# A graph layer's second and third matrix in parts of the TensorE array, by sets of four node tiles

## What is computed

```python
def gnn(x, edge_src, edge_dst, w, W1, W2, W3):      # W1 64x256, W2 32x64, W3 256x32
    agg = segment_sum(x[edge_dst], edge_src)
    y = agg + w * x
    h = relu(y @ W1.T)
    h = relu(h @ W2.T)
    h = relu(h @ W3.T)
    return h + x

x = x + gnn(layernorm(x), ...)
xn = layernorm(layernorm(x)) * gamma + beta
logits = xn @ Wr + br ; top 2 of 8, softmax of the two
for e in range(8): y += (gelu(xn @ W1[e] + b1[e]) @ W2[e] + b2[e]) * w_full[e]
out = x + y
```

## Time and profile before

| | us |
|---|---|
| median of 3 runs | 478.48 |
| lowest and highest | 477.6, 479.87 |
| span of the profiled execution, first to last instruction | 472.4 |
| third stage, first L1141 to L1224 | 157.13 to 216.15 |
| TensorE busy over the span | 380.4 (81%) |
| VectorE, ScalarE, GpSimd busy | 294.7, 222.6, 135.4 |

### The profile page before, as it was taken

The page is one execution under the profiler, slowest core; times in us unless marked ns, Lnnn a source line. Parts: engine busy times, 40 slices in busy tenths (PEclk is TensorE's granted clock), DMA queues, the critical chain, the costliest instruction groups (busy, mean ns, idle before and its releaser), DMA issues.

```text
span 472.4 us, 12881 instructions
## 1 busy us (share of the span) xinstructions
PE 380.4 (81%) x4344; PEld 346.1 (73%) x4345; DVE 294.7 (62%) x704; ACT 222.6 (47%) x351; POOL 135.4 (29%) x241
## 2 busy tenths in 40 slices
PE   0895598999998889980449999999999999999200
PEld 0684498999998667770349999999999999999100
DVE  2886998999994753568945444445444444444853
ACT  2475576888885274560025444444444444443000
POOL 3050000000000500000054665665666665653200
PEclk9987589999999977875559999999999999999755
DMA  9620299999999269930011222212222222215899
GB/s 202 154 54 3 40 183 199 214 220 222 216 222 200 63 241 362 375 116 0 0 58 58 77 70 72 72 67 67 75 69 73 72 67 67 75 60 135 207 228 310
DMA packets 112696, 62.15 MB, mean 132 GB/s; under 512 B 86625, under 2 KB 106743, under 8 KB 112544
## 3 DMA queue, kind: packets, MB, share of 16 engines
q1 hardware_dynamic: 101168, 41.80, 36.6%
q0 software_dynamic: 6272, 14.93, 10.2%
q10 hardware_dynamic: 5232, 5.12, 3.7%
HBM read 27.70 MB, written 13.64 MB: 88 GB/s over the span
## 4 chain that ended last, share of the span: by engine, by line
PE 70%; DMA 9%; DVE 8%; ACT 5%; issue 4%; SPq 3%; POOL 0%; ACTq 0%; DVEq 0%; POOLq 0%
PE psum L918 20%; PE psum L929 19%; PE psum L790 9%; PE psum L781 7%; DMA w_sb<-pair_rows 3%; PE psum L837 3%; PE psum L859 3%; PE psum L907 2%; DMA at<-cts 2%; DMA b_rows<-in_L_ffn_b_dram 2%; PE psum L721 1%; DMA pair_rows<-yb,scol 1%; SPq L288 1%; PE psum L712 1%; ACT cts L591 1%
## 5 line engine op out<-in xcount | busy, mean ns | idle before, releaser
L918 PE MATMUL psum<-xgT,w_now 128*128 128x128 f32 x832 | 103.2, 278 | 0.0
L918 PEld LDWEIGHTS psum<-xgT,w_now 128*128 128x128 f32 x832 | 98.8, 195 | 0.2 <-issue 0.2
L929 PE MATMUL psum<-w_sb,hT 128*128 x416 | 98.4, 380 | 0.0
L591 ACT CAST cts<-psum 128x1000 bf16<-128x1000 f32 x100 | 78.4, 815 | 23.7 <-PE psum L781 23.3
L929 PEld LDWEIGHTS psum<-w_sb,hT 128*128 128x128 f32 x416 | 75.1, 190 | 8.3 <-issue 0.3
L679 ACT ACTIVATE hT<-up 128x512 f32<-128x512 f32 x52 | 32.8, 630 | 97.7 <-DVE up L1347 97.7
L790 PE MATMUL psum<-z,at 125*128 (+1 forms) x1875 | 71.0, 195 | 3.2 <-DMA at<-cts 3.2
L668 ACT COPY w_now<-w_sb 128x1024 f32 x52 | 54.4, 1046 | 34.5 <-DVEq L1312 21.9
L790 PEld LDWEIGHTS psum<-z,at 125*128 125x128 bf16 x1875 | 65.9, 100 | 3.8 <-DMA at<-cts 2.1
L1347 DVE TENSOR_TENSOR up<-psum,b1T 128x512 f32<-128x512 f32 x52 | 36.0, 692 | 47.8 <-PE psum L918 47.8
L492 POOL DMA_INDIRECT pair_rows<-yb,scol x52 | 52.0, 999 | 46.9 <-issue 33.6
(11 more groups left out here) (228 smaller groups left out, 347.8 us busy)
## 6 DMA issues: line engine op xcount, KB each, us to landing
w_sb<-in_L_ffn_W_dram SPq DMA_DIRECT2D x2, 4096.0 KB, 20.4
token_rows<-tok SPq DMA_DIRECT2D x5, 560.0 KB
tok<-pair_rows SPq DMA_DIRECT2D x5, 560.0 KB
w_sb<-pair_rows SPq DMA_DIRECT2D x5, 560.0 KB
out_dram<-res ACTq DMA_DIRECT2D x5, 560.0 KB
res<-in_x_dram ACTq DMA_DIRECT2D x3, 560.0 KB
res<-in_x_dram SPq DMA_DIRECT2D x2, 560.0 KB
b_sb<-in_L_ffn_b_dram SPq DMA_DIRECT2D x1, 1024.0 KB, 23.8
```

What stands on the lines that cost most here:

```text
L591: act.copy(cts[:, par, :, d0:d0 + nw * WD].rearrange("p h (b d) -> p b h d", b=nb), psum[:, bank:bank + nb, 0:wb * WC].rearrange("p b (d h ...
L918: last = pe.matmul(psum[:, j % 2, c * P:(c + 1) * P], w1_now[:, j % 2, k, c * P:(c + 1) * P], xgT[:, j % 2, k, :], start=(k == 0), stop=(k ...
L929: last = pe.matmul(psum[:, 4 + j % 2, 0:D], hT[:, j % 2, k, :], w2_sb[:, ds(e, 1), k, :].rearrange("p a h -> p (a h)"), start=(k == 0), st ...
```

## The change

The 25 tiles go in seven sets, six of four tiles and one of one, in place of five groups of five. In a set:

- the second layer is four matmuls of 125 columns, one for each tile; each has the 64x32 weights and writes its own 32 rows of PSUM bank 4 (rows 0 to 31, 32 to 63, ...), so each uses its own 32 columns of the array;
- one ReLU reads these 128 rows x 125 columns (before: 32 rows x 375 and x 250);
- the third layer is four matmuls of 256 columns, each with 32 rows of `h2T` and the same 32 rows of `gW3T`, each into its own bank (6, 7, 0, 1); `gW3T` now holds the matrix four times, one below the other; VectorE waits for the last of the four;
- the residual takes two tiles in an instruction (125x512), from two banks;
- tokens go two tiles to a bank, through the banks 2 and 5, and are copied two at a time (128x500);
- `deviation2` of set k-1 stands ahead of `relu_y` of set k+1 on ScalarE.

`top_two` takes 24 tiles and then one. At the start POOL copies `gW3` four times side by side (a new instruction that waits for the loads and stands ahead of the constants that follow on POOL), in place of two memsets; TensorE waits for it before its first transpose, and turns 128 columns of it in place of 32.

```diff
+SL = P // F2
+SETS = -(-NT // SL)
...
-        H3 = (6, 7, 0)
-        TURN = (1, 2)
-        ALL_BUT_LAST = NT - G
+        H3 = (6, 7, 0, 1)
+        TURN = (2, 5)
+        MLP = 4
+        ALL_BUT_LAST = (SETS - 1) * SL
...
-            pool.memset(gW3T[:], 0.0).then_inc(c_more, 1)
-            pool.memset(h2T[:].rearrange("p t n -> p (t n)"), 0.0).then_inc(c_more, 1)
+            pool.wait_ge(L["small"], 64)
+            pool.tensor_copy(gW3_sb[:], gW3_in[:].unsqueeze(2).broadcast_to([P, KD, SL, F2])).then_inc(gW3_spread, 1)
...
+            def relu_h2(k):
+                n = len(sets[k]) * F2
+                act.wait_ge(h2_psum, k + 1)
+                act.activation(h2T[0:n, :], psum[0:n, MLP, 0:T], ACT.Relu).then_inc(h2_sb, 1)
...
+            def copy_tokT(k):
+                for i, ts in enumerate(pairs_of(k)):
+                    n, t0 = len(ts), 2 * i
+                    act.wait_ge(tokT_psum, 2 * k + i + 1)
+                    act.copy(tokT[:, :, t0:t0 + n, :], psum[:, TURN[i], 0:n * KD * T].rearrange(
+                        "p (t k n) -> p k t n", t=n, k=KD)).then_inc(tokT_sb, 1)
...
+            pe.wait_ge(gW3_spread, 1)
...
+            def second_layer(k):
+                pe.wait_ge(yT_sb, k + 1)
+                for i in range(len(sets[k])):
+                    last = pe.matmul(psum[i * F2:(i + 1) * F2, MLP, 0:T], gW2T[:], y1T[:, i, :], start=True, stop=True)
+                last.then_inc(h2_psum, 1)
+
+            def third_layer(k):
+                pe.wait_ge(h2_sb, k + 1)
+                if k >= 1:
+                    pe.wait_ge(h3_used, 2 * k)
+                for i in range(len(sets[k])):
+                    last = pe.matmul(psum[0:T, H3[i], 0:D], h2T[i * F2:(i + 1) * F2, :], gW3T[i * F2:(i + 1) * F2, :],
+                                     start=True, stop=True)
+                last.then_inc(h3_psum, 1)
...
+            def residual_set(k):
+                dve.wait_ge(h3_psum, k + 1)
+                for i, ts in enumerate(pairs_of(k)):
+                    n, rows = len(ts), slice(ts[0], ts[-1] + 1)
+                    dve.scalar_tensor_tensor(res[:, rows, :], psum[0:T, H3[2 * i]:H3[2 * i] + n, 0:D], 0.0,
+                                             res[:, rows, :], ALU.max, ALU.add).then_inc(h3_used, 1)
+                dve.wait_ge(h3_used, 2 * k + len(pairs_of(k)))
...
-            for k in range(NG + 1):
+            for k in range(SETS + 1):
                 if k >= 1:
                     scales2(k - 1)
-                if k < NG:
-                    residual_group(k)
+                if k < SETS:
+                    residual_set(k)
                     moments2(k)
```

More of the change, by code:

```diff
@@ L813, in _ @@
             pe.wait_ge(L["few"], 80)
[L815 to L818, removed]
-                for h, (t0, t1) in enumerate(halves):
-                    for t in range(t0, t1):
-                        last = pe.transpose(psum[0:F1, 4 + h, (t - t0) * T:(t - t0 + 1) * T], y1[:, g * G + t, :], ident[0:T, 0:T])
-                    last.then_inc(yT_psum, 1)
-            def second_layer(g):
-                for h, (t0, t1) in enumerate(halves):
-                    pe.wait_ge(yT_sb, g * 2 + h + 1)
-                    pe.matmul(psum[0:F2, 4 + h, 0:(t1 - t0) * T], gW2T[:], y1T[:, t0:t1, :].rearrange("p t n -> p (t n)"),
-                              start=True, stop=True).then_inc(h2_psum, 1)
@@ L830, in third_layer @@
-            def third_layer(g):
-                for i in range(len(H3)):
-                    if g >= 1:
-                        pe.wait_ge(h3_used, (g - 1) * len(H3) + i + 1)
-                    for t in range(2 * i, min(2 * i + 2, G)):
-                        pe.wait_ge(h2_sb, g * 2 + (1 if t < 3 else 2))
-                        c = (t % 2) * D
-                        last = pe.matmul(psum[0:T, H3[i], c:c + D], h2T[:, t, :], gW3T[:], start=True, stop=True)
-                    last.then_inc(h3_psum, 1)
@@ L848, in turn_tokens, with logits @@
+            def turn_tokens(k):
+                for i, ts in enumerate(pairs_of(k)):
+                    if k >= 1:
+                        pe.wait_ge(tokT_sb, 2 * k + i - 1)
+                    for a, t in enumerate(ts):
+                        pe.wait_ge(tok_norm, t + 1)
+                        for h in range(KD):
+                            c = (a * KD + h) * T
+                            last = pe.transpose(psum[:, TURN[i], c:c + T], tok[:, t, h * P:(h + 1) * P], ident[0:T, 0:T])
                     last.then_inc(tokT_psum, 1)
-            def logits(g):
-                if g == 0:
+            def logits(k):
+                if k == 0:
@@ L863, in _ @@
             second_layer(0)
-            for k in range(NG + 2):
-                if k + 1 < NG:
+            for k in range(SETS + 2):
+                if k + 1 < SETS:
                     turn_y(k + 1)
```

128 lines of the change are left out of this document (57 added, 71 removed).

## The result

The changed kernel took **485.25 us** (median of four runs, 484.14 to 489.76), the kernel before 478.04 (four runs, 476.81 to 479.87): a ratio of **1.0174, 95% interval 1.0107 to 1.0241**. I had forecast 472.5 and a range that ended at 483. The sign was wrong too.

A forecast was written before the change was run, and what follows sets the result against it. The third stage was taken to hang on TensorE, with a chain through VectorE and ScalarE close behind. From 478.5 us, 6.1 less in that stage and 0.1 more at the start gave 472.5 us, range 466 to 483.

The forecast's parts named there:

- The sum 478.5 - 6.1 + 0.1: Whole kernel: time before, less the third stage's gain, plus 0.1 at the start, giving 472.5 us.
- not 6.1: Third stage: its end at 210.0 against 216.15, so 6.1 us less.
- The overlap: Third stage: four matmuls last five records, not eight or two; third layer 1.17 us, second 0.5.
- rival 2: Second and third layers: all four matmuls run beside each other, 467.8 us in all; chance 0.2.
- Steps of 4.8 and 9.2: Third stage: 4.8 us a step at full clock, set by the chain; 9.2 at half, set by TensorE.
- my lower end: TensorE in the third stage: a set costs 3.6 us if four parts of the array run fully beside each other.
- The clock: 40%: Third stage: 40% of it at half clock, as before, giving 5.93 us a step.
- rival 3: Third stage: TensorE stays at half clock for want of long 128-row streams, 486 us in all; chance 0.1.
- my 64%: Third stage: share at half clock at which it would end as before, s = 0.64.
- The start: Kernel start: POOL's copy costs nothing to 0.3 us, wider transposes 0 to 0.2; 0.1 taken for both.
- The end: Third stage after its last third layer: 12.8 us at full clock, 14 at half, 13.4 taken; 6.4 less.
- A cost of changing shape: TensorE in the third stage: 15 more shape switches at 0 to 0.33 us, 0 to 5 us; none taken.

The follow-up runs named there:

- e2: The kernel before with two unused SBUF tiles that shift the buffers behind them about as the change does: 486.31 us, ratio 1.0207.
- e3: The changed kernel with 992 unused bytes that put `cts` and `at` back at their old places: 477.92 us, no ratio.
- f4: The kernel before with 32 unused bytes ahead of `cts` alone: 480.23 us.
- h2: The changed kernel with 224 unused bytes ahead of `cts`, a multiple of 256 but not 512, timed with twelve runs: 474.89 us, ratio 1.0017.
- h3: The changed kernel with 992 unused bytes that put `cts` back at its old place, timed again with twelve runs: 477.0 us, ratio 0.9994.
- g1: The changed kernel with 480 unused bytes ahead of `cts` alone, which puts it at a multiple of 512: 483.02 us, ratio 1.0148.
- f2: The kernel before with its third layer reading only the 32 rows that aren't zero, with nothing overlapping: 492.41 us, ratio 1.0273.
- h1: The kernel before with 32 unused bytes ahead of `cts` alone, timed again with more runs: 489.38 us, ratio 1.0306.

## Why the prediction was wrong, point by point

**The step that failed first: a term put at nothing.** The sum 478.5 - 6.1 + 0.1 gives the aggregation no term at all. It is untouched in its instructions and took 7.0 us more, and that carried the sign. I looked at what the change adds and moves on the engines and queues, and at POOL and SP, but never at where the buffers come to lie, though a shrunken `h2T` stands in the diff. e2, e3 and f4 show it; h2 and h3 show that with it gone nothing of the slowdown is left. But nothing of the forecast gain appears either, and that is the second step that failed.

**The third stage: 1.8 us shorter, not 6.1.** From its start to the first third layer 4.4 us were measured (174.34 to 178.77) and 3.9 forecast, for the six steps to the last third layer 38.3 and 35.6, for the end 14.5 and 13.4. The largest miss is in the steps, and the clock made it; the next points take the terms one by one.

**The overlap: 1.17 and 0.5 us for third and second layer, a middle value.** Mis-sized, on the safe side. Measured 0.64 and 0.35 at the full clock, 1.16 and 0.58 at half: near rival 2, whose sum had 0.47 and 0.2. I had assumed that records start in the order of the matmuls, so that the second half of one blocks the next. They don't: the four first halves start within 0.04 us, and the four second halves 0.3 later. The Trainium skill, TensorE: Matmul & The Clock Gate, Part 3, had the right answer, and I gave it 0.2 because no row bore it out for f32. Its 3.07x for four tiles of 512 columns compares with 0.233 / 0.080 = 2.9 here, with 256.

**Steps of 4.8 and 9.2.** Measured 4.20 and 7.6 (g1, third layers 7.59 and 7.60 apart; 7.0 for the last two steps, which turn no y), rival 2's were 4.45 and 7.3. TensorE's own sum for a set was 3.6 in my lower end; 4.20 is what a step takes with no wait in it at all: logits 1.84, tokens 0.91, `y` 0.46, third layer 0.65, second 0.34. The logits came out at 0.115 a record, I had 0.105. I also misread the waiting in a step of before: the one from 188.40 to 196.37 turns no y, so of its 7.97 us not 0.9 but 1.4 is waiting.

**The clock: 40%.** The term that took back the gain: 80 to 93% in nine profiles of the unfilled changed kernel. I had the mechanism as rival 3, and argued against it with "turned y and tokens in one piece are more of a short step". f2 shows that the rows driven count, and the 128-row pieces of a step weren't enough. With the measured steps the break-even is not my 64%: g1 at 92% took 59.1, as before at 40%. The prediction did name the share of the clock as what would spoil its number most.

**Rival 3's 486 us is nearly the measured 485, and wrong all the same.** It put 7 us into the third stage. The third stage was 1.8 us shorter than before; the 7 us were elsewhere. Its mechanism was right, its price wrong, and its total came out by luck.

**What held.** The start: TensorE's first transposes at 13.39 (13.43 before), POOL's copy 0.40 us at 12.04 under the cover of VectorE; in seven of the thirteen profiles with the new start the counts begin between 50.2 and 51.3, against 50.7 before; the other six had a late first stage, as two of the five with the old start had. The end: forecast 13.4, or 14 at half clock, measured 14.5, with `top_two` over 24 tiles at 5.3 (5.1) without a pause and over one at 2.9 (2.9). A cost of changing shape: none to be seen in the step of h3, where each group of instructions follows without a pause, so the value of 0 was right. SP and the stages behind: 0.1 us.

**What the parts come to.** 7.0 for the aggregation less 1.8 for the third stage are 5.2 us, of the 7.2 between the medians. The other 2 aren't placed; the first stage's clock, which differs from execution to execution by up to 10 us, is the likely one.

## What to carry to other kernels

An edit that changes the size of one buffer moves all that are allocated behind it: compare the places of the operands of every DMA before and after, and keep the source of a transposing DMA with rows of 256 bytes at a multiple of 256 bytes of its partition (0.8 us on top of 3.5 for each here, and 7 us of the stage). Packing small matmuls into parts of the array shortened them 2.9 times here, but what a stage gains is decided by the clock that it is then granted: read the share at half clock in both traces before the lengths of the instructions. And a total that agrees with a theory proves nothing until the stage named by the theory shows the difference.

## What the runs showed of the hardware that I had not expected

- 32 bytes of offset of a transposing DMA's source cost 7.4 us over 50 DMAs (f4: 3.5 to 4.3 us to landing, 106.4 to 113.8 us of aggregation); 128 bytes are as bad as 32, 256 as good as 512.
- TensorE, busy for 92% of the time, was kept at 1.2 GHz for nearly a whole stage when its third layer drove 32 rows in place of 128 (94% against 40%), and 2.4 GHz again for 30.7 us on end when 1.1 us of each 5.3 went into 128-row matmuls that compute nothing anyone reads.
- Four f32 matmuls of 32 rows, two records each, take 0.64 us together, where five of 128 rows took 2.33: four first halves side by side, then four second halves.
- The first stage's clock alone moves a run by 10 us (counts from 50.2 to 61.6 us), with either start, and between two executions of one kernel (f4 50.7, h1 61.1).
